# Post-norm attention and expert layers on one core: the first gate logits one slot later, a first-layer step in their place, and another order at the head of slot 14 and of the tail

## What is computed

```python
# x: 8 sequences of 256 tokens, 128 wide, bf16
q, k, v = (x @ W.T + b for (W, b) in ...)          # 16 heads of 64
q, k = apply_rope(q, k)
attn = softmax(einsum('bhqd,bhkd->bhqk', q, k) * 64 ** -0.5)
x = layernorm(x + merge_heads(attn @ v) @ Wo.T + bo)
gates = softmax(x @ gate_w)                        # 8 experts
topk_g, topk_i = top_k(gates, 2); tok_w = topk_g.sum(-1)
sel = (topk_i[:, :, None] == arange(8)).any(1)
h = gelu(einsum('nd,edh->enh', x, w1) + b1)        # 64 hidden units an expert
y = einsum('enh,ehd->end', h, w2) + b2
x = layernorm(x + einsum('end,ne,n->nd', y, sel, tok_w))
```

## Time and profile before

| | us |
|---|---|
| median of 3 runs | 223.0 (222.32 to 223.11) |
| profiled execution | 222.24 |
| its span | 220.4 |
| TensorE busy | 173.0 (79%) |
| VectorE busy | 180.7 (82%) |
| ScalarE busy | 169.4 (77%) |
| GpSimd busy | 141.3 (64%) |
| mean granted TensorE clock | 0.991 of 2.4 GHz |

### The profile page before, as it was taken

The page is one execution under the profiler, slowest core; times in us unless marked ns, Lnnn a source line. Parts: engine busy times, 40 slices in busy tenths (PEclk is TensorE's granted clock), DMA queues, the critical chain, the costliest instruction groups (busy, mean ns, idle before and its releaser), DMA issues.

```text
span 220.4 us, 5283 instructions
## 1 busy us (share of the span) xinstructions
PE 173.0 (79%) x1839; PEld 122.4 (56%) x1839; DVE 180.7 (82%) x522; ACT 169.4 (77%) x357; POOL 141.3 (64%) x123
## 2 busy tenths in 40 slices
PE   1879678686767886887788679758697998999991
PEld 0223345464645664666567456636484675777781
DVE  6989969958796987898789969797989788486483
ACT  3878786777589978976997899688567989649624
POOL 6070777398989799798979997899850033021514
PEclk9999999889999999999999999999999999999999
DMA  6233423131214322121313121212120000001012
GB/s 234 88 82 85 103 70 83 31 82 36 63 37 122 105 67 62 36 62 38 86 32 77 41 63 40 61 47 53 48 51 1 4 3 3 0 3 48 0 52 95
DMA packets 13002, 12.63 MB, mean 57 GB/s; under 512 B 3152, under 2 KB 11952, under 8 KB 12976
## 3 DMA queue, kind: packets, MB, share of 16 engines
q1 hardware_dynamic: 12832, 12.03, 20.5%
q10 hardware_dynamic: 144, 0.26, 0.3%
HBM read 2.73 MB, written 1.05 MB: 17 GB/s over the span
## 4 chain that ended last, share of the span: by engine, by line
PE 27%; DVE 26%; POOL 18%; ACT 7%; issue 7%; DMA 3%; POOLq 0%; DVEq 0%; ACTq 0%
DVE row_max L1212 10%; POOL by_sin L1042 9%; POOL by_cos L1042 8%; DVE roped L1171 8%; PE ps_o L600 5%; PE ps_s L565 5%; DMA qk<-mT_sb 3%; PE ps_t L455 3%; PE ps_m L507 3%; DVE o_sb L1235 3%; PE ps_s L403 2%; ACT raw L830 2%; ACT probs L865 2%; ACT x L877 2%; PE ps_o L476 2%
## 5 line engine op out<-in xcount | busy, mean ns | idle before, releaser
L865 ACT ACTIVATE probs<-ps_t 128x512 bf16<-128x512 f32 x128 | 76.7, 616 | 27.8 <-PE ps_t L455 27.5
L1212 DVE TENSOR_REDUCE row_max<-ps_s 128x2 bf16<-128x512 f32 x120 | 80.3, 674 | 4.8 <-PE ps_s L403 3.0
L1042 POOL TENSOR_TENSOR by_cos<-raw,in_b 128x1024 bf16<-128x1024 bf16 x25 | 53.0, 2122 | 22.1 <-DVE roped L1171 19.8
L830 ACT ACTIVATE raw<-ps_m,bqk 128x256 bf16<-128x256 f32 x128 | 53.6, 489 | 6.0 <-PE ps_m L388 5.9
L403 PE MATMUL ps_s<-qk 128*128 128x256 bf16 x218 | 41.7, 278 | 18.6 <-DVE row_max L1212 16.1
L1042 POOL TENSOR_TENSOR by_sin<-raw,in_b 128x1024 bf16<-128x1024 bf16 x25 | 53.0, 2122 | 0.0
L455 PE MATMUL ps_t<-qk 128*128 128x256 bf16 x256 | 49.3, 276 | 1.8 <-DMA qk<-mT_sb 1.7
L476 PE MATMUL ps_o<-v_sb,probs 128*128 128x65 bf16 x512 | 36.2, 195 | 1.0 <-DVE row_max L1212 0.6
L476 PEld LDWEIGHTS ps_o<-v_sb,probs 128*128 128x128 bf16 x512 | 31.7, 98 | 6.8 <-issue 1.7
L388 PE MATMUL ps_m<-in_b 128*128 128x256 bf16 x128 | 27.1, 304 | 9.4 <-DMA in_b<-in_packed_b 4.3
L403 PEld LDWEIGHTS ps_s<-qk 128*128 128x128 bf16 x218 | 14.6, 98 | 25.4 <-issue 10.9
(11 more groups left out here) (136 smaller groups left out, 250.5 us busy)
## 6 DMA issues: line engine op xcount, KB each, us to landing
qk<-roped SPq DMA_DIRECT2D x128, 64.0 KB, 2.0
in_b<-in_packed_b SPq DMA_DIRECT2D x1, 768.0 KB, 5.8
out<-y_sb SPq DMA_DIRECT2D x3, 256.0 KB, 2.2
in_f<-in_packed_f SPq DMA_DIRECT2D x1, 586.0 KB, 4.0
in_b<-in_packed_b SPq DMA_DIRECT2D x1, 512.0 KB, 4.4
in_b<-in_packed_b ACTq DMA_DIRECT2D x1, 256.0 KB, 3.7
qk<-mT_sb SPq DMA_DIRECT2D x16, 4.0 KB, 1.7
bv_rep<-in_repeated_bv SPq DMA_DIRECT2D x1, 256.0 KB, 2.9
```

Source lines behind the costliest of these rows:

```text
L830: last = nc.scalar.activation(raw[:, u % 2, g, a, half, :], ps_m[bank][:, half * S:half * S + S], ACT.Identity, bias=bqk[:, a, chunk:chunk ...
L865: nc.scalar.activation(probs[:, h % 4].rearrange("p c s -> p (c s)"), ps_t[h % 2][:], ACT.Exp, scale=DH ** -0.5).then_inc(exp_done, 1)
L1042: last = nc.gpsimd.tensor_tensor(by[:, g].rearrange("p a h s -> p (a h) s"), raw[:, u % 2, g].rearrange("p a h s -> p (a h) s"), table[:]. ...
L1212: nc.vector.tensor_reduce(row_max[:, u % 2, h % 4, h // 4, :], of_head[:].rearrange("p (t s) -> p t s", s=S), AX_X, ALU.max, negate=True). ...
```

## The change

- `hidden(2)` takes the place of `logits(0)` in slot 13; it writes ps_m[1] and waits for that bank's reader. The value product that next takes ps_m[1] waits for `keep_hidden(2)`, which stands on ScalarE behind exp(13, 6).
- `logits(0)` stands at the head of slot 14 and writes ps_m[0]. Its routing steps 1 and 2 move to slot 14 on VectorE, behind `invert_sums(13, 3)`, and `gate_exp(0)` behind `read_x1T(1)` on ScalarE.
- In slot 14 the scores for the maxima of heads 5 and 6 of unit 15 stand behind `scores(14, 0)`, `times_v(13, 7)` and `logits(0)` instead of ahead of them.
- The first-layer steps move up by one place: 3 and 4 in slot 14, 5, 0 and 1 in slot 15, none at the beginning of the tail. All but step 2 use bank ps_s[(k + 1) % 2].
- In the tail, `spread_weights(2)` stands between the two turns of the last output, `spread_weights(3)` before `hidden(6)`, and `hidden(7)` behind `experts_out(0, 0)`.

```diff
-        LOGIT_BANK = (1, 1, 0)
+        LOGIT_BANK = (0, 1, 0)
...
+        def hidden_bank(k):
+
+            return ps_m[1] if k == 2 else ps_s[(k + 1) % 2]
...
             def hidden(k):
                 tc, c = k // NE, k % NE
                 pe.wait_ge(x1T_ready, max(tc, 1))
-                if k in (2, 3):
+                if k == 2:
+                    take(1, h_kept, 1)
+                    pe.wait_ge(split_step, 10)
+                elif k in (3, 4):
                     pe.wait_ge(max_done, UNITS * UH)
-                    pe.wait_ge(split_step, 10)
                 elif k < 6:
-                    pe.wait_ge(h_kept, k + 3 if k < 2 else k - 3)
+                    pe.wait_ge(h_kept, {5: 2, 0: 3, 1: 4}[k])
...
                 find_scores(0)
-                find_scores(1)
+                if T != 14:
+                    find_scores(1)
...
+                if T == 14:
+                    logits(0)
+
+                if T == 14:
+                    find_scores(1)
                 if s["attend"]:
                     scores(T, 1, it)
                 if T in (13, 14):
                     turn_x1(T - 13)
                 if T == 15:
-                    hidden(4)
+                    hidden(5)
...
                 if T == 13:
-                    logits(0)
+                    hidden(2)
                 if T == 15:
-                    hidden(5)
+                    hidden(0)
...
                 if T == 14:
-                    hidden(2)
+                    hidden(3)
...
                 if T == 15:
-                    hidden(0)
+                    hidden(1)
...
                 if T == 14:
-                    hidden(3)
+                    hidden(4)
...
-            hidden(1)
             spread_weights(0, 1)
             turn_o(LAST, 0, 0)
+            spread_weights(2)
             turn_o(LAST, 1, 0)
-            spread_weights(2)
+            spread_weights(3)
             hidden(6)
-            spread_weights(3)
+            experts_out(0, 0)
             hidden(7)
-            experts_out(0, 0)
             spread_weights(4, 5)
...
                 if T == 15:
-                    keep_hidden(3)
+                    keep_hidden(4)
                     gate_exp(1)
...
+                if T == 14:
+                    gate_exp(0)
...
                 if T == 15:
-                    keep_hidden(4)
+                    keep_hidden(5)
...
                     exp(T, 6, it)
+                if T == 13:
+                    keep_hidden(2)
                 if T == 14:
-                    keep_hidden(2)
-                if T == 15:
-                    keep_hidden(5)
+                    keep_hidden(3)
...
                     exp(T, 7, it)
-                if T == 13:
-                    gate_exp(0)
...
                     invert_sums(T - 1, 3, it)
+                if T == 14:
+                    route(0, 1)
+                    route(0, 2)
...
                     normalise(T, 1, it)
-                if T == 13:
-                    route(0, 1)
-                    route(0, 2)
```

More of the change, by code:

```diff
@@ L564, in hidden @@
                 for part in range(3):
-                    mm = nc.tensor.matmul(ps_s[k % 2][:], w1_p[:, part, c * P:c * P + P],
+                    mm = nc.tensor.matmul(hidden_bank(k)[:], w1_p[:, part, c * P:c * P + P],
                                           x1T[:, tc * TC:tc * TC + TC], start=(part == 0), stop=(part == 2))
@@ L859, in keep_hidden @@
                 act.wait_ge(h_ready, k - 1)
-                nc.scalar.copy(h_sb[:, k - 2, :], ps_s[k % 2][:]).then_inc(h_kept, 1)
+                nc.scalar.copy(h_sb[:, k - 2, :], hidden_bank(k)[:]).then_inc(h_kept, 1)
             def exp(u, h, it):
@@ L986, in _ @@
                     act.wait_ge(h_ready, k + 1 if k >= 6 else k + 5)
-                    of_k = ps_s[k % 2][:]
+                    of_k = hidden_bank(k)[:]
                 if k >= HG:
```

## The result

The changed kernel took 226.67 us (median of 4 runs, 224.43 to 226.82) against 222.81: a ratio of 1.0136 with a 95% interval of 1.0095 to 1.0177: 1.4% slower, clear of the noise. The forecast was 223.7, range 222.4 to 225.0. Timed twice more beside other kernels, the same code gave 226.01 (1.0147, 1.0073 to 1.0222) and 224.76 (1.0062, 1.0017 to 1.0106): over its 18 executions it scatters from 223.3 to 227.2.

A forecast was written before the change was run, and what follows sets the result against it. TensorE's solid work was taken to bound the end, with VectorE's chain setting the head of slot 14. Head 0.53 plus tail 0.19 gave +0.72 us, 223.7 us from a median of 223.0, range 222.4 to 225.0.

The forecast's parts named there:

- The copy's wait, +0.23: Slot 13: value(15,1,1) waits for keep_hidden(2) on ScalarE, delaying the maxima of (15,3) by 0.23 us, bounds 0.05 and 0.35.
- the 0.53 of the sum: Head of slot 14: copy's wait and route steps together delay the turn of unit 15's maxima by 0.53 us.
- the rival by which it costs nothing: Head: copy done early or route steps in opened gaps, so only the tail's cost remains, 223.1 us; chance 16%.
- The route steps in the chain, +0.32: Slot 14: two route steps in VectorE's solid chain before the maxima of (15,7) add 0.32 us, bounds 0.25 and 0.47.
- The earlier first score buys nothing: Slot 14: exp of (14,0) starts 1.3 us earlier, but TensorE still waits for VectorE, so no gain.
- The slots only shift: Turn of the maxima to end of slot 15: TensorE's stretch, shifted by 0.53 us and not shortened.
- `hidden(1)` costs nothing where it stood: Start of the tail: its 0.65 us lay in the shadow of route steps and wtT; removing it gives 0.
- the mechanism as a rival: Tail: TensorE's clock falls behind the longer hole of about 1.6 us before the spreads, 225.4 us; chance 6%.
- The price of the fall, 1.7 us: Tail: a clock fall behind the hole costs 1.7 us, the full clock missing from 42 to 46.
- The tail's order, +0.19: Tail: spread_weights(2) waits for the first weigh, uncovered by the second eight transposes, 0.19 us of new idle.
- a pace set by ScalarE: Slots 14 and 15: exps set the pace, so earlier exps and one copy fewer give 222.7 us; chance 8%.
- no stall at `experts_out(0,0)`: Tail: the rival had experts_out(0,0) stall, with all behind it, for 0.5 us more, 224.2 us; chance 12%.

The follow-up runs named there:

- e1: The changed kernel with hidden(1) put back in the tail between slot 15 and the spreads, all else as changed: 223.19 us, 1.0008.
- e2: The changed kernel with six unread 128 x 512 matmuls on TensorE filling the hole between slot 15 and the spreads: 222.99 us, 1.0034.
- e8: The kernel before with unread matmuls in TensorE's longest holes of slots 1, 2, 3, 5, 7, 9 and 11: 221.33 us, 0.9926.
- e7: The changed kernel with the hole filled, route(0,1) and route(0,2) off VectorE's chain and the gate's exp behind exp(14,3): 222.71 us, 0.9996.

## Why the prediction was wrong

- **The copy's wait, +0.23.** Right: `value(15,1,1)` came at 168.48, 0.96 after the first value product for 0.79 before (+0.17), and the maxima of (15,3) 0.97 after the maxima of (15,2) for 0.77 (+0.20). The step for the logits adds 0.06 in front of it (2.76 us to the first value product for 2.70), so the head's delay is 0.52 for the 0.53 of the sum, and the rival by which it costs nothing is out.
- **The route steps in the chain, +0.32.** Right: they stand at 172.07 and 172.29 with the maxima 0.15 behind; from the maxima of (15,3) to the turn it is 4.34 us for 4.07 (+0.27), and taking them out gave 0.40.
- **The earlier first score buys nothing.** Right: TensorE waits 1.12 us for the same `normalise`, longer than the 0.42 of the earlier trace rows.
- **The slots only shift.** Off by 0.11 us, in favour of the change; the last copy ahead of exp(15,7) is gone, which may be why, but no run shows it. That the stretch is TensorE's alone was too strong: one step fewer gave 0.25 of 0.65.
- **`hidden(1)` costs nothing where it stood, so removing it gives nothing.** This is the step that failed. The time of the step was indeed in the shadow; but it had kept TensorE's idle time at 0.8 us, and at 1.5 the clock fell. The sum put the removed step at nothing; the tail took 3.05 us more, 2.9 of them at the low clock. The prediction saw the hole, named the mechanism as a rival, and gave it 6%, because the hole was shorter than the two of the earlier trace rows and dense work stood before it. Neither protects: eight of nine profiles with this hole fell. Nor is one profile a rule: holes of 1.4 us in front of 84 and 125 kept the clock in the profile of before, and in that of e1 low stretches stood behind them, from 86 to 90 and from 126 to 132.
- **The price of the fall, 1.7 us.** Near for a short one (1.5 to 1.6 measured: tails of 16.83 to 17.02 for 15.30 and 15.45), but in two profiles of the changed kernel it lasted twice as long and cost 2.9 and 3.0. That it was near is partly luck: it was read off the stretch from 42 to 46, where 1.7 us of full clock went missing and GpSimd's products came no later. In the tail, where TensorE has no hole, what goes missing is lost. Taken from the one case that the trace showed, it was no upper bound, and the range's top, 225.0, was below even this rival's own 225.4.
- **The tail's order, +0.19.** Right (+0.14 to +0.21), but what it does to a fallen clock wasn't thought of.
- **The other rivals.** Of a pace set by ScalarE nothing was seen, and no stall at `experts_out(0,0)` stands in its waits.

What stays open: what decides between a fall of 3.5 and one of 7 us (the order of the tail seems to shift the odds; the same order showed both), why the fillers shorten the front at a clock of 1.00, and whether what stands right behind the hole, spreads of 32 rows and then transposes, takes part in the fall: it is there in all nine profiles with the hole.

## What to carry to other kernels

Work in the shadow of a wait isn't free to remove: on TensorE it may be what holds the clock. Before moving work out of a hole, add up how long the engine then idles, look at several profiles and not at one, and where any shows a fall behind the like of it, put it into the sum and not beside it. Price it by what follows: here it cost 1.5 to 3.0 us in front of work that is all TensorE's, and nothing visible where other engines set the pace. Where a hole can't be closed, a few matmuls into a bank whose next writer overwrites it fill it: six of them took 2.9 us off this tail. In the front such fillers gave 0.7 to 1.0%, but mostly not by the clock that they were put in for: a gain doesn't prove the theory that led to it.

## What the runs showed of the hardware

- The low clock came behind single idle times of 1.4 to 2.0 us, but not behind each, and where TensorE is less busy also behind shorter ones: in the profile of the changed kernel behind 1.02 us, with the eight matmuls that took 0.62 us in e2 taking 0.96, in e8 behind 1.02 and 0.76 close together, and in e7, from 28 on, with no idle time over 0.76 us in the 11 us before it. The same hole in the same program had the fall behind it in one execution and not in another. (The Trainium skill, "TensorE: Matmul & The Clock Gate", Part 1, ties the clock to how busy the array has recently been and says that where the transition lands varies from run to run. These executions agree, and go further: whether a fall comes at all varied.)

```profile
32.66 0.21 PE L519 MATMUL ps_m<-in_b,ones_row 1*128 1x128 bf16 x1 [1.02 <-ACT raw L841]
32.80 0.96 PE L521 MATMUL ps_m<-in_b,bv_rep 128*128 128x128 bf16 x8
```

- The fillers did something else that was not foreseen, and it is the larger part of their gain. The wait of the scores for the row of maxima that comes by DMA was shorter: for unit 7 that DMA landed 2.4 us after its issue in the profile of before and 1.7 in that of e8. The same DMA inside the gaps from 56.30 and 137.96 on landed after 2.7 and 2.6 us in before and after 1.7 in e8 at the second; at the first it took 2.8 in e8 too, and there the gap stayed at 6.65 us. From 97.28 to 103.57 the first products of GpSimd are 6.29 us apart in before, 6.2 to 6.8 in the others without front fillers, and 5.8 in all six with them; from 137.96 on it is 6.2 to 6.9 and again 5.8. Why, the runs don't tell.
